# First 128 queries of the first projection in a bank of their own, value products evicted ahead of `h`, the second set's reciprocals turned in step 10

## What is computed

```python
h = _group_norm(x, gn_w, gn_b)                       # 8 groups of 16 channels
q = jnp.einsum('oc,bcn->bon', qw, h) + qb[None, :, None]
k = jnp.einsum('oc,bcn->bon', kw, h) + kb[None, :, None]
v = jnp.einsum('oc,bcn->bon', vw, h) + vb[None, :, None]
attn = jnp.einsum('bcn,bcm->bnm', q, k) / jnp.sqrt(jnp.asarray(C, x.dtype))
attn = jax.nn.softmax(attn, axis=-1)
out = jnp.einsum('bnm,bcm->bcn', attn, v)
out = jnp.einsum('oc,bcn->bon', pw, out) + pb[None, :, None]
return x + out.reshape(B, C, H, W)
```

## Time and profile before

| | |
|---|---|
| median of 3 runs | 140.49 us (140.24 to 140.89) |
| the profiled execution's own time | 140.34 us |
| its span, first to last instruction | 138.4 us |
| granted TensorE clock over the span | 1.00 |
| busy: PE, DVE, ACT, POOL | 129.9, 99.5, 64.9, 26.1 us |
| idle of PE from 5.0 to 29.8, from 29.8 to 43.0, from 43.0 to 134.9 us | 0.37, 3.19, 0.00 us |

### The profile page before, as it was taken

How to read it: one execution, slowest core, us unless ns; L and a number is a source line. 1 busy time by engine, 2 the same in 40 slices (tenths; PEclk the granted TensorE clock), 3 DMA queues, 4 the chain that set the end, 5 groups by cost and what they waited for, 6 DMA issues and landing times.

```text
span 138.4 us, 2200 instructions
## 1 busy us (share of the span) xinstructions
PE 129.9 (94%) x743; PEld 112.5 (81%) x743; DVE 99.5 (72%) x172; ACT 64.9 (47%) x112; POOL 26.1 (19%) x33
## 2 busy tenths in 40 slices
PE   5999999997878999999999999999999999999990
PEld 5986888885656888999898888899988889998880
DVE  0577788989999678979687789756987798330222
ACT  4044689655556574634347735354544334412000
POOL 5053050750202033300032063000030012003000
PEclk9999999999999999999999999999999999999999
DMA  4960000002998699569781998699825998997512
GB/s 133 279 271 0 0 5 0 10 31 63 203 211 200 166 208 206 154 149 211 158 219 47 207 207 179 206 203 209 199 97 122 207 207 222 216 216 169 167 38 76
DMA packets 9566, 21.00 MB, mean 152 GB/s; under 512 B 2362, under 2 KB 4052, under 8 KB 9556
## 3 DMA queue, kind: packets, MB, share of 16 engines
q1 hardware_dynamic: 8816, 20.59, 61.2%
q10 hardware_dynamic: 740, 0.28, 0.7%
HBM read 4.07 MB, written 2.11 MB: 45 GB/s over the span
## 4 chain that ended last, share of the span: by engine, by line
PE 87%; DVE 8%; issue 3%; POOL 0%; DVEq 0%; POOLq 0%
PE ACC L375 36%; PE S L322 10%; PE S L323 9%; PE S L326 9%; PE S L266 5%; PE A L302 5%; DVE s_sb L654 3%; PE S L350 2%; PE ACC L350 2%; DVE blocks L663 2%; PE ACC L402 1%; PE A L402 1%; DVE g_lo L628 1%; DVE bn L579 1%; PE A L278 1%
## 5 line engine op out<-in xcount | busy, mean ns | idle before, releaser
L375 PE MATMUL ACC<-pT,v 128*128 128x128 f32 (+1 forms) x320 | 53.3, 317 | 0.0
L654 DVE TENSOR_SCALAR_CACHE_REDUCE s_sb<-S,row_term 128x1024 f32<-128x1024 f32 x32 | 41.0, 1281 | 16.4 <-PE S L326 16.0
L375 PEld LDWEIGHTS ACC<-pT,v 128*128 128x128 f32 x320 | 46.4, 191 | 3.9
L500 ACT ACTIVATE s_sb<-s_sb,rowmin 128x1024 f32<-128x1024 f32 x32 | 36.9, 1152 | 20.9 <-DVE s_sb L654 19.8
L663 DVE STREAM_TRANSPOSE blocks<-s_sb 128x1024 f32<-128x1024 f32 x28 | 34.7, 1239 | 0.0
L322 PE MATMUL S<-h_hi,g_hi 128*128 128x512 f32 x64 | 29.2, 457 | 0.3 <-issue 0.3
L323 PE MATMUL S<-h_lo,g_hi 128*128 128x512 f32 x64 | 25.1, 393 | 0.0
L326 PE MATMUL S<-h_hi,g_lo 128*128 128x512 f32 x64 | 19.9, 392 | 0.0
L808 POOL TENSOR_TENSOR xb<-rden_bc,xb 128x512 f32<-128x512 f32 (+1 forms) x7 | 8.4, 1198 | 49.8 <-DVE rden_bc L683 42.3
L326 PEld LDWEIGHTS S<-h_hi,g_lo 128*128 128x128 f32 x64 | 12.0, 188 | 2.8
L322 PEld LDWEIGHTS S<-h_hi,g_hi 128*128 128x128 f32 x64 | 12.1, 189 | 2.2 <-issue 0.4
(11 more groups left out here) (90 smaller groups left out, 102.9 us busy)
## 6 DMA issues: line engine op xcount, KB each, us to landing
pT<-blocks SPq DMA_DIRECT2D x112, 128.0 KB, 2.5
rden_bc<-row_store SPq DMA_DIRECT2D x6, 256.0 KB, 3.4
x_sb<-x SPq DMA_DIRECT2D x1, 1024.0 KB, 6.3
out<-xb SPq DMA_DIRECT2D x8, 128.0 KB, 2.8
out<-xb SPq DMA_DIRECT2D x4, 256.0 KB, 2.9
x_sb<-x SPq DMA_DIRECT2D x2, 256.0 KB, 3.0
x_sb<-x SPq DMA_DIRECT2D x1, 512.0 KB, 4.1
w_in<-weights ACTq DMA_DIRECT2D x2, 128.0 KB, 3.5
```

The costliest lines, as they stand in the source:

```text
L375: last = pe.matmul(to, v[:, b % 3, t, :], probs[:, :, t, :], start=(t == 0), stop=(t == KT - 1))
L500: act.activation(s_sb[:, c % 3, :], s_sb[:, c % 3, :], ACT.Exp, bias=rowmin[:, c % CH:c % CH + 1], scale=-1.0, accum_out=den[:, n % 2, k:k ...
L654: dve.tensor_scalar(s_sb[:, c % 3, :], S[:, c % 2, :], row_term[:, b % 2, i:i + 1], None, ALU.add, ALU.min, accum_out=rowmin[:, i:i + 1]). ...
```

## The change

Six edits:

1. The first projection goes in two pieces: queries 0 to 127 into `ACC` bank 1 (`project_first_g(0, P)`), then the first value tiles, then queries 128 to 511 into `ACC` bank 0. `h_lo` of the first half is made in two pieces to match.
2. ACT evicts the products of the value weights ahead of `h_hi` of batch 0. The three `keep_warm` matmuls among those products go, four more are put after them.
3. In ACT's list the first copy of value tiles stands ahead of the rounding of `g` 128 to 511, which no longer waits for `g_lo` of the first 128. In the scores of step 0 each wait stands at the matmul that needs it.
4. On DVE, `wa_lo` is made ahead of the statistics of batch 1's first half.
5. In step 3, both halves of the pair copy of step 1 are ACT's; DVE has only that of step 0.
6. The reciprocals of set 1 are turned by PE in step 10 (step 7 before), copied and sent by ACT in step 11 (7 before), and broadcast by a DMA that ACT issues in step 12 (SP before, behind the moves of set 1).

```diff
@@ -77,6 +77,10 @@
+        def turn_step(n):
+            return CH + 2 if n == 1 else FIRST[n + 1] + 1
@@ -217,7 +221,6 @@
             move_set(1)
-            spread_rows(1)
             store_set(0)
@@ -237,7 +240,7 @@
                 if b > 1:
-                    pe.wait_ge(rows_ready, 2 * (b - 1))
+                    pe.wait_ge(rows_ready, sum(turn_step(n) < CH * (b - 1) for n in range(SPREAD_BY_DMA)))
                 pe.matmul(A0[:, 0:1], deviation[:, :], chan[:, 0:1], start=True, stop=True).then_inc(dmean_psum, 1)
@@ -253,11 +256,8 @@
                 pe.matmul(A1[:, PROD_G:PROD_G + 1], w_in[:, KW, :], cols[:, QB:QB + 1], start=True, stop=True)
-                keep_warm(1)
                 pe.matmul(A1[:, PROD_ROW:PROD_ROW + 1], w_in[:, QW, :], cols[:, KB:KB + 1], start=True, stop=True)
-                keep_warm(1)
                 pe.matmul(A1[:, PROD_C:PROD_C + 1], cols[:, QB:QB + 1].to_broadcast([P, P]), cols[:, KB:KB + 1], start=True, stop=True)
-                keep_warm(1)
                 pe.matmul(A1[:, PROD_B:PROD_B + 1], w_in[:, PW, :], cols[:, VB:VB + 1], start=True, stop=True)
@@ -265,23 +265,33 @@
-            def project_g(b, f):
-                to = ACC[:, 0, :] if b == 0 and f == 0 else A1[:, :]
-                cs = slice(BANK * f, BANK * (f + 1))
-                if b == 0 and f == 0:
+            def project_first_g(c0, c1):
+                cs, k = slice(c0, c1), 1 if c0 == 0 else 0
+                if c0 == 0:
                     pe.wait_ge(wa_hi_ready, 1)
                     pe.wait_ge(wa_lo_ready, 1)
+                    pe.wait_ge(h_hi_ready, 1)
+                pe.matmul(ACC[:, k, cs], wa_hi[:, :], h_hi[:, 0, cs], start=True, stop=False)
+                pe.matmul(ACC[:, k, cs], wa_lo[:, :], h_hi[:, 0, cs], start=False, stop=False)
+                if c0 == 0:
+                    pe.wait_ge(h0_lo_first, 1)
                 else:
-                    pe.wait_ge(v_ready, VP * b if f == 0 else VP * b + 2)
-                    pe.wait_ge(row_ready, VP * b if f == 0 else VP * b + 2)
+                    pe.wait_ge(h0_lo_ready, 1)
+                pe.matmul(ACC[:, k, cs], wa_hi[:, :], h_lo[:, 0, cs], start=False, stop=True).then_inc(g_first_psum if c0 == 0 else g_psum, 1)
+            def project_g(b, f):
+                cs = slice(BANK * f, BANK * (f + 1))
+                pe.wait_ge(v_ready, VP * b if f == 0 else VP * b + 2)
+                pe.wait_ge(row_ready, VP * b if f == 0 else VP * b + 2)
                 pe.wait_ge(h_hi_ready, HALVES * b + f + 1)
-                pe.matmul(to, wa_hi[:, :], h_hi[:, b % 2, cs], start=True, stop=False)
-                pe.matmul(to, wa_lo[:, :], h_hi[:, b % 2, cs], start=False, stop=False)
+                pe.matmul(A1[:, :], wa_hi[:, :], h_hi[:, b % 2, cs], start=True, stop=False)
+                pe.matmul(A1[:, :], wa_lo[:, :], h_hi[:, b % 2, cs], start=False, stop=False)
                 if b == 0:
...
                     pe.wait_ge(h_lo_ready, b)
-                pe.matmul(to, wa_hi[:, :], h_lo[:, b % 2, cs], start=False, stop=True).then_inc(g_psum, 1)
+                pe.matmul(A1[:, :], wa_hi[:, :], h_lo[:, b % 2, cs], start=False, stop=True).then_inc(g_psum, 1)
@@ -306,10 +316,8 @@
                     pe.wait_ge(g0_hi_first, 1)
-                    pe.wait_ge(g0_lo_first, 1)
                     pe.wait_ge(wa_lo_ready, 1)
-                    pe.wait_ge(h_hi_ready, HALVES)
-                    pe.wait_ge(h0_lo_ready, HALVES)
+                    pe.wait_ge(h0_lo_ready, 1)
                 elif i == 0 or c == 1 or i == GC:
@@ -319,8 +327,14 @@
                     ks = slice(BANK * f, BANK * (f + 1))
+                    if c == 0:
+                        pe.wait_ge(h_hi_ready, f + 1)
                     pe.matmul(S[:, c % 2, ks], g_hi[:, qs], h_hi[:, b % 2, ks], start=True, stop=False)
+                    if c == 0:
+                        pe.wait_ge(h0_lo_ready, f + 1)
                     pe.matmul(S[:, c % 2, ks], g_hi[:, qs], h_lo[:, b % 2, ks], start=False, stop=False)
+                if c == 0:
+                    pe.wait_ge(g0_lo_first, 1)
                 for f in range(HALVES):
@@ -328,7 +342,7 @@
                 pe.wait_ge(rden_ready, n + 1)
-                pe.wait_ge(gvar_ready, min(FIRST[n + 1] // CH + 2, B))
+                pe.wait_ge(gvar_ready, min(turn_step(n) // CH + 2, B))
                 if n > 0:
@@ -387,8 +401,8 @@
                     to = (ACC[:, f, :] if c < SETS[0] else (A1, A0)[f])
-                    if c == 0 and f == 0:
-                        pe.wait_ge(g_lo_ready, 1)
+                    if c == 0:
+                        pe.wait_ge(g_lo_ready if f == 0 else g0_lo_first, 1)
                     if c == DIRECT and f == 0:
@@ -411,9 +425,10 @@
             value_products()
-            keep_warm(5)
-            project_g(0, 0)
+            keep_warm(9)
+            project_first_g(0, P)
             value_tiles(0, 0)
+            project_first_g(P, BANK)
@@ -428,8 +443,9 @@
                     value_tiles(b, 2)
-                if c - 1 in FIRST[1:LS]:
-                    turn_rden(FIRST.index(c - 1) - 1)
+                for n in range(SPREAD_BY_DMA):
+                    if c == turn_step(n):
+                        turn_rden(n)
                 if i == 6 and b < L:
@@ -474,15 +490,14 @@
                 if b == 0 and f == 0:
-                    act.wait_ge(g0_lo_first, 1)
                     act.activation(g_hi[:, P:BANK], ACC[:, 0, P:BANK], ACT.Identity, bias=g_bias).then_inc(g_hi_ready, 1)
...
             def round_first_g():
-                act.wait_ge(g_psum, 1)
+                act.wait_ge(g_first_psum, 1)
                 act.wait_ge(wpv_ready, 1)
-                act.activation(g_hi[:, 0:P], ACC[:, 0, 0:P], ACT.Identity, bias=g_bias).then_inc(g0_hi_first, 1)
+                act.activation(g_hi[:, 0:P], ACC[:, 1, 0:P], ACT.Identity, bias=g_bias).then_inc(g0_hi_first, 1)
@@ -521,6 +536,9 @@
                 act.copy(pair_T[:, 0:PT, c % 2, :], frm.rearrange("p (t q) -> p t q", t=PT)).then_inc(pair_ready[0], 1)
+                if c == 1:
+                    act.wait_ge(tp_psum, HALVES * (k + 1))
+                    act.copy(pair_T[:, PT:KT, 1, :], ACC[:, 1, :].rearrange("p (t q) -> p t q", t=PT)).then_inc(pair_ready[1], 1)
@@ -529,15 +547,15 @@
             act.mul(wa_hi[:, :], product_a, -SCALE).then_inc(wa_hi_ready, 1)
-            for f in range(HALVES):
-                normalize_hi(0, f, f + 1)
             act.wait_ge(prod_psum, 2)
...
             act.activation(out_bias[:, :], A1[:, PROD_B:PROD_B + 1], ACT.Identity, bias=cols[:, PB:PB + 1]).then_inc(bias_ready, 1)
+            for f in range(HALVES):
+                normalize_hi(0, f, f + 1)
             round_first_g()
+            copy_v(0, 0)
             round_g(0, 0)
-            copy_v(0, 0)
@@ -557,8 +575,13 @@
                     copy_v(b + 1, 0)
-                if i == 7 and c - 1 in FIRST[1:LS]:
+                if i == 7 and c > CH and c - 1 in FIRST[1:LS]:
                     copy_rows(FIRST.index(c - 1) - 1)
+                if c == turn_step(1) + 1:
+                    copy_rows(1)
+                if c == turn_step(1) + 2:
+                    act.wait_ge(rows_stored[1], 16)
+                    act.dma_start(rden_bc[:, 1, 0:P * GC], row_store[1:2, 0:P * GC].to_broadcast([P, P * GC])).then_inc(rows_spread[1], 16)
                 if c - 2 in range(SETS[0]):
@@ -612,11 +635,11 @@
-            def split_h0(f):
+            def split_h0(f, c0, c1, done):
                 dve.wait_ge(h0_ready[f], 1)
                 dve.wait_ge(h_hi_ready, f + 1)
-                cs = slice(BANK * f, BANK * (f + 1))
-                dve.tensor_tensor(h_lo[:, 0, cs], h[:, cs], h_hi[:, 0, cs].bitcast(F32), ALU.subtract).then_inc(h0_lo_ready, 1)
+                cs = slice(c0, c1)
+                dve.tensor_tensor(h_lo[:, 0, cs], h[:, cs], h_hi[:, 0, cs].bitcast(F32), ALU.subtract).then_inc(done, 1)
@@ -714,17 +737,18 @@
             group_var(0)
-            half_stats(1, 0)
             dve.wait_ge(wa_hi_ready, 1)
...
                .then_inc(wa_lo_ready, 1)
+            half_stats(1, 0)
             dve.wait_ge(cols_loaded, 16)
...
             dve.tensor_scalar(h[:, cs0], x_sb[:, 0, cs0], gscale[:, :], gshift[:, :], ALU.mult, ALU.add).then_inc(h0_ready[0], 1)
-            split_h0(0)
-            split_h0(1)
+            split_h0(0, 0, P, h0_lo_first)
+            split_h0(0, P, BANK, h0_lo_ready)
+            split_h0(1, BANK, N, h0_lo_ready)
             dve.wait_ge(wpv_ready, 1)
@@ -743,8 +767,8 @@
                 drain_scores(c)
-                if c - 2 in range(SETS[0]):
-                    copy_pair(c - 2)
+                if c == 2:
+                    copy_pair(0)
                 if c > 0 and not is_direct(c - 1):
```

(4 more changed lines are left out.)

## The result

The changed kernel takes 141.21 us (median of 17 runs, 140.87 to 142.68) against 140.72 us (17 runs, 140.05 to 141.19): a ratio of 1.0052, 95% interval 1.0034 to 1.0070, so 0.73 us slower (0.48 to 0.98). The ratio is not that of the two medians, which lie only 0.49 apart; it is near that of the means, 141.34 and 140.62. The forecast was +0.37, a time of 140.7 and at most 141.2. The side was right; the size is twice what was forecast by the ratio (0.12 more by the medians), and the time lies 0.01 above the range. The profiled execution took 141.22 us for a span of 139.2.

The account below looks back on a forecast made before the run. PE was taken to bound the kernel to 29.8 us and from 43.0 us on, DVE between. The sum was 140.34 - 0.13 (start) + 0.50 (step 11) = 140.71, say 140.7 us, range 140.1 to 141.2.

Parts of the forecast that it names:

- Start: Start of the kernel up to step 0's value tiles: a gain of 0.16 us, of which 0.13 is left at drain 6.
- So `row_term` moves 0.16, from 13.13 to 12.97: Step 0: DVE's `row_term` comes 0.16 us earlier because ACT's rounding of `g` 128 to 511 starts at 11.71, not 11.87.
- Gain carried on: 0.16: End of the start: PE's value tiles of step 0 begin 0.16 us earlier, at 13.26 instead of 13.42.
- Steps 3 and 4: Pair copy moved from DVE to ACT: PE loses 0 to 0.07 us at the direct unit; DVE's freed 0.69 buys nothing.
- Drain 6: Sign of being right, at the hand-over from PE to DVE: drain 6 at 29.7 us.
- Step 7 and step 10: Taking the turn out of step 7 gives PE nothing; putting it in step 10 costs PE 0.11 us.
- Step 11: PE waits about 0.6 us at turn 2 for ACT's row copy behind `h_hi`; the value unit starts 0.5 later before the gain.
- Broadcast: Step 12, issued by ACT: lands at 54.2 to 54.8 us, before divide 1 needs it at 55.5; cost 0.
- No stall: Rival at step 11: the row copy is done before PE arrives, total some 140.0 to 140.2 us; chance 0.06.
- DVE's copy is worth its size: Rival for drains 3 to 5: DVE's 0.69 us leaves the chain, total 140.0, or 139.5 without the stall; chance 0.04.
- narrow fp32r matmuls run like fp32: Rival at the first projection: 0.224 us per 128 columns, total 141.05, or 142.5 if 384 columns are slow too; chance 0.10.

Follow-up runs that it names:

- b_again: The kernel before, unchanged, profiled a second time; 140.40 us.
- h1: g1 with ACT's eviction of `out_bias` put back behind `h_hi`, the other value products staying ahead; 139.72 us, ratio 0.9956 to the kernel before.
- e4: The changed kernel with POOL's `xb` of batch 0 held back until `h_lo` is complete; 141.51 us, ratio 1.0073 to the kernel before.
- f2: Changed kernel, edit 6 undone, POOL's `xb` held until `h_lo` is complete, second projection piece and its rounding ahead of value tiles and their copy; 140.61 us, ratio 1.0001.
- g2: g1 with edit 5 undone, so DVE again copies the second half of step 1's pair; 140.68 us, ratio 1.0014 to the kernel before.
- g1: f2 with seven `keep_warm` instead of nine and without the wait that held back POOL's `xb`; 140.86 us, ratio 1.0020 to the kernel before.
- e1: The changed kernel with edit 6 undone (turn of set 1 back in step 7); 140.53 us, ratio 1.0018 to the kernel before.
- e3: The changed kernel with set 1's row copy ahead of `h_hi` of batch 2 in ACT's list; 141.07 us, ratio 1.0037 to the kernel before.
- e2: The kernel before with edit 6 alone; 140.90 us, ratio 1.0041 to the kernel before.

## Why the prediction was right and where it was wrong

**The sum.** Relative to `gvar` and against b_again, the unit of step 11 comes 0.79 us later (40.28 - 39.49). Of that 0.21 arose at the start and 0.56 in step 11; measured was 0.73. The prediction had -0.13 and +0.50. Of the 0.42 between the 0.79 and the forecast's 0.37 the start has 0.34 and step 11 has 0.06. That the time of 141.21 ended above the range has a second reason: the sum was made against one execution of 140.34, and the kernel before, in the runs beside the changed one, had a median of 140.72.

**Start: wrong.** The step that failed is "So `row_term` moves 0.16, from 13.13 to 12.97", and with it "Gain carried on: 0.16". In place of a gain of 0.13 to 0.16 the runs show a loss of 0.21 against a kernel before with its load in time. PE's part was not misjudged: the narrow matmuls are 0.11 apart (10.34 to 10.45), and `g_hi` 0 to 127 is at 3.52 after `gvar`, against 3.99 in the profile that was read (3.74 in b_again). The 0.056 that the prediction took from the Trainium skill, "TensorE: Matmul & The Clock Gate", section "Wait — 56ns, not 53.3ns?", is not seen here, where each matmul loads new weights. Two terms failed, and together they make the 0.34.

- The price of a wait removed, 0.10 in this kernel (6.45 - 6.35). Edit 2 was costed as three small evictions on ACT. Who waits for `out_bias` was not asked. It is POOL's `xb`, which in b_again began at 10.67, near the end of `h_lo` (9.60 to 11.00), after 0.88 of waiting for ACT. Released at 9.0 it starts as soon as POOL has made its half of `h`, at 9.85, and the last piece of `h_lo` takes 0.80 longer. h1 shows that this line of edit 2 does it, e4 that no other property of the change makes `h_lo` long.
- The baseline, 0.25. The row counted from was late by a late load, and the gain that the prediction gave to edit 4 (`gshift` at 8.29 for 8.48) is there only when that load is late.

The order of the start was in the sum, and the sum was right about it. The prediction had ACT's rounding of `g` 128 to 511 begin 0.16 earlier than in its profile (11.71 for 11.87). It begins 4.91 after `gvar` there and 4.77 in e4: 0.14. `row_term` moves from 6.17 to 6.04, by 0.13; only the collision brings it back to 6.15. Against b_again (4.66 for the rounding) the same order is a loss of 0.11. What the prediction did not look for is a better order: f2, with the second projection and its rounding ahead of the value tiles, is 0.42 earlier.

The Trainium skill has a rule for the first term, "SBUF — State Buffer", section "Who interferes with whom": a VectorE instruction with two SBUF inputs contends with a GpSimd instruction that reads SBUF, and the one that issues second is blocked until the other is done. The traces agree in the main: `h_lo` reads `h` and `h_hi` and grows from 0.71 to 1.51 where `xb` is under way, and in h1, where `h_lo` is first, `xb` grows from 1.13 to 1.55 and `h_lo` of half 1 takes 0.68. But in the changed kernel both grow: `xb` takes 1.59 there, and the first two pieces of `h_lo`, which end inside its record, take no longer than in e4, where `xb` is held back. This rule spoke against the change, and the prediction did not weigh it.

**Steps 3 and 4: right.** PE loads for the direct unit 0.07 after the second copy ends (22.90 + 0.59 = 23.49, load at 23.56), and 1.12 after the first copy starts, where it was 1.04: 0.08 later, for a forecast of 0 to 0.07. g2 against g1 puts the whole edit at 0.04. Drain 6 starts at 30.11, not at the 29.7 of the prediction; 0.29 of that is this profile's later `gvar`.

**Step 7 and step 10: right.** From the value tiles of step 0 to the unit of step 11 it is 33.24 us in e1, with the turn in step 7, and 33.38 in e3, with the turn in step 10 and no wait: nothing gained there, the turn's 0.11 paid here. In the changed kernel the wait swallows it.

**Step 11: right, slightly small.** 0.56 for 0.50: the turn loads 0.35 after the copy starts, in the changed kernel and in e2 (47.04 to 47.39, 46.58 to 46.93). The term was 0.06 too small.

**Broadcast: right.** Divide 1 starts 0.84 later than in the earlier trace rows, as does the unit of step 11 (47.53 against 46.69); nothing is added between.

**Rivals.** "No stall" and "DVE's copy is worth its size" are refuted by e2 and g2, "narrow fp32r matmuls run like fp32" by the pitch of 0.11. The range was too narrow at the top: the only case in it in which the start loses is that of slow narrow matmuls. POOL was not looked at, and the before was known from one profile.

## What to carry to other kernels

When an eviction goes earlier, follow its semaphore to every engine that waits for it, not only the one that it was moved for; an instruction released early runs beside something new, and with DVE and POOL that can double an instruction. Where two chains end within 0.1 us of each other, taking away one shows only that 0.1: the cost of a collision is known when the other chain has been shortened as well. Count places from a common row, and take a second profile of the kernel before when a row of the first hangs on a load.
